# Layer 1's self attention with queries in rows: softmax in rows, probabilities turned by TensorE, three pairs of PSUM banks and a new order in part three

## The chip, the cores and the metric

One core of a Trainium2 chip. The metric is device time in microseconds (us) of one execution. The kernel before takes 1746.66 us, the median of 3 runs (1746.36 to 1750.59).

## The reference, cut to what matters

A decoder of two blocks for 16 sequences of 256 tokens of 128 values, with a second input (a context of 64 tokens of 96 values for each sequence). Every layer adds its result to its input and normalizes the sum. Layer 0 has a causal attention (16 heads of 8), an attention on the context (8 heads of 16) and a mixture of 64 experts; layer 1 has the attention that changes here (16 heads of 64), an attention on the context (16 heads of 64) and a small attention of 8 heads in place of a feed-forward network.

```python
def _L1_attn_ref(x, W_qkv, b_qkv, W_out, b_out):        # x: 16 x 256 x 128
    qkv = (x @ W_qkv + b_qkv).reshape(B, S, 3 * 16, 64)
    Q, K, V = qkv[:, :, :16], qkv[:, :, 16:32], qkv[:, :, 32:]
    scores = jnp.einsum('bqhi,bkhi->bhqk', Q, K) / jnp.sqrt(64.0)
    scores = scores + jnp.triu(jnp.full((S, S), -10000.0), k=1)
    probs = jax.nn.softmax(scores, axis=-1)
    vals = jnp.einsum('bkhi,bhqk->bqhi', V, probs).reshape(B, S, 16 * 64)
    return vals @ W_out + b_out

x = _layernorm(x + _L0_attn_ref(x, ...))
x = _layernorm(x + _L0_xattn_ref(x, ctx_768, ...))
x = _layernorm(x + _L0_ffn_ref(x, ...))
x = _layernorm(x + _L1_attn_ref(x, ...))                 # the layer that changes
x = _layernorm(x + _L1_xattn_ref(x, ctx_768, ...))
x = _layernorm(x + _L1_ffn_ref(x, ...))
```

## The kernel before

**Parts.** Part one is the causal attention and the context attention of layer 0, the router and some folding of weights; part two runs the experts; part three is the whole of layer 1. The change touches part three, and a few constants that are prepared earlier.

**Streams and the written order.** Part three works on two sequences at a time, A and B, in eight repetitions of one body. The work of a body is six streams of steps (`phase3_streams`): for each of the two sequences one of the three layers in a row (`main`), one that sums what the experts left, normalizes it and begins layer 1 for the sequence of the next body (`front`), and one of value projections (`values`). The string `TURNS3` says from which stream the next step is taken, A and B being the main streams, C and D the fronts, E and F the values. `AHEAD3` says how many steps of each stream belong to the next repetition. These ahead steps run for the first bodies in front of the loop, the others of the last bodies behind it. Between lies the loop, from 765.95 to 1688.5 us in the profiled execution, with seven repetitions; in front of it is a stretch from 679.78.

Every engine goes through the same list of steps in the same order (`tensor_step`, `scalar_step`, `vector_step`, `pool_step`, and `transfer_step` for SP, which issues the DMAs), and does its share of each step. An engine that waits in one step holds back all its later steps.

**The steps of layer 1's self attention for one sequence.** XT turns the input. Q and K project queries and keys, two pairs of heads a step; ScalarE adds the bias and writes them, features in rows, to `qt` and `kt`; V projects the values. C casts `qt` (ScalarE) and `kt` (VectorE, L1214) to bf16. There are eight pairs of heads.
- S, eight steps: scores with queries in rows, bf16 (L706) plus a mask (L713), 128x1024 in one pair of PSUM banks; VectorE takes the largest of each row (L1279). They serve only for this maximum. N turns the negated maxima with four small matmuls.
- T, four rounds of two steps: the scores again, now in fp32 with keys in rows (L805), to which a matmul with `shift` (L800) adds the negated maxima and one more (L794) the mask; ScalarE takes the exponential of 128x1024 (L1143) into `prob`.
- P, four steps: the values times the probabilities (L896), and the sums of the probabilities through a matmul with ones (L883) into a bank of its own; ScalarE copies the products (L1150).
- D: VectorE forms the reciprocals of the sums and splits them into three bf16 parts. B, two steps: TensorE spreads them over the features with `spread_b` (L950), and VectorE multiplies the products by them (L1303). W is the output projection (L969), and L the norm.

The context attention of layer 1 (L1X) already has queries in rows in the kernel before: its T steps turn probabilities with eight transposes of 128x128 (L811), and ScalarE copies them (L1134). GpSimd adds the residuals (L1477) and forms the norms' reciprocal roots (L1457, L1460); VectorE applies the norms (L1202).

**PSUM.** `Ledger` hands out units of PSUM in turn from rings. In part three there are six units, two of them pairs of banks (ring Q: S, T and B), one bank for P's products (O), one for the sums (D) and two for all projections (M). In one body Q has 60 fills, M 48, O 10 and D 2. An engine that fills a unit waits until the fill before it is read (`may_fill`).

```python
UNIT_BANK = (0, 2, 4, 5, 6, 7)
RINGS = {"p1": {"Q": (0, 1), "O": (2, 3), "M": (4, 5)},
         "p3": {"Q": (0, 1), "O": (2,), "D": (3,), "M": (4, 5)}}
AHEAD1, AHEAD3 = (22, 17, 6, 0, 0, 0, 0), (16, 22, 15, 15, 4, 4)
```

Of the kernel before, what the change touches and what calls it, by code (L numbers as in the profile page):

```python
# [50 lines left out]
ROUNDS_T = {L0: 4, L0X: 1, L1: 4, L1F: 2}  # L51
# [13 lines left out]
def project_steps(a, s):  # L65
    st = lambda kind, *n: [(kind, a, s, i) for i in n]
    scores = len(S_STEPS[a])
    if a is L1:
        out = st("Q", 0, 1) + st("C", 0) + st("S", 0, 1, 2, 3)
    elif a is L0X:  # L70
        out = st("Q", 0) + st("C", 0) + st("S", 0)
    else:
        out = st("Q", 0) + st("C", 0) + st("S", 0) + st("V", 0) + st("S", *range(1, scores))
    return out + st("N", 0)


def head_steps(a, s):
    out = []
    for g in range(ROUNDS_T[a]):
        out += [("T", a, s, g, k) for k in range(2 if a is L1 else 1)]  # L80
        if g:
            out.append(("P", a, s, g - 1))
# [32 lines left out]
def early_steps(s):  # L115

    st = lambda kind, *n: [(kind, L1, s, i) for i in n]
    return [("XT", L1, s, 0)] + st("K", 0, 1, 2, 3) + st("Q", 2, 3) + st("C", 1) + st("S", 4, 5, 6, 7)


def phase3_streams():
    front = lambda s: [("Z", "F", s, 0), ("Y", "F", s, 0), ("L", "F", s, 0)] + early_steps(s)
    values = lambda s: [("V", L1, s, i) for i in range(4)]
    main = lambda s: (project_steps(L1, s) + head_steps(L1, s)
# [7 lines left out]
TURNS3 = ("B4 A2 D2 A3 D B A B D B D2 A2 B A F B2 A C D5 C F A B A C A B2 A C B D A C5 B A D B2 E A F B3 A B2 "  # L132
          "A2 B2 F A D2 A2 E B E A C A2 B A B A B A C B A B4 A2 B C E B2 A B A B C A2 B C2 A3 B3 A B2 A B2 A B "
          "A B2 A B A B A6 B A B A")
AHEAD1, AHEAD3 = (22, 17, 6, 0, 0, 0, 0), (16, 22, 15, 15, 4, 4)


def interleaved(streams, turns, aheads):
# [16 lines left out]
UNIT_BANK = (0, 2, 4, 5, 6, 7)  # L155
UNITS = len(UNIT_BANK)
RINGS = {"p1": {"Q": (0, 1), "O": (2, 3), "M": (4, 5)},
         "p3": {"Q": (0, 1), "O": (2,), "D": (3,), "M": (4, 5)}}


def fills(step):
# [6 lines left out]
    if kind == "P":  # L168
        if a is L1:
            return ["D", "O"] if step[3] == 0 else ["O"]  # L170
        return ["O"] if step[3] == 0 else []
    if kind == "B":
        return ["Q"]
    if kind in ("D", "E", "L", "C", "CK", "RN", "RL", "Z", "Y") or kind == "W" and step[3]:
        return []
# [3 lines left out]
def tilings(step):  # L179
# [3 lines left out]
    if kind in ("C", "CK", "D", "E", "L", "RN", "RL", "Z", "Y"):  # L183
        return ()
    if kind in ("S", "T") and a in (L0, L1):
        return ((32, 128), (32, 32)) if narrow else ((64, 128), (64, 64))
    if kind in ("S", "T") and a is L1X:
# [3 lines left out]
    if kind == "P":  # L191
        return {L1: ((128, 64), (128, 32)), L0X: ((128, 64),)}.get(a, ((128, 32),))
# [40 lines left out]
def decoder_program(nc, inp, out):  # L233
    ctx = ExitStack()
    with ctx:
# [29 lines left out]
        ones_g = sb("ones_g", [128, 2, 4, 32])  # L265
        spread_b = sb("spread_b", [128, 8, 128], BF16)
        part_cols = sb("part_cols", [128, 2])
# [12 lines left out]
        sel_m = w_early[:, 0:256].bitcast(BF16).rearrange("p (g k) -> p g k", g=4)  # L280
# [7 lines left out]
        peak_w = [w_shared[:, 256 * s:256 * s + 256].bitcast(BF16).rearrange("p (n j c) -> p n j c", n=2, j=2) for s in AB]  # L288
# [41 lines left out]
        qb = pair("qb", [128, 8, T], BF16)  # L330
# [4 lines left out]
        xt_x = [t[:, 0, :] for t in qt]  # L335
        by_query = [[flat(t[:, 4 + 2 * n:6 + 2 * n, :]).rearrange("p (h k) -> p h k", h=16) for n in AB] for t in prob]
# [9 lines left out]
        shift = pair("shift", [128, 2, T], BF16)  # L346
        shift_n = pair("shift_n", [128, 384], BF16)
        rpart = pair("rpart", [128, 128], BF16)
        rdiag = pair("rdiag", [128, 2, 128], BF16)
# [89 lines left out]
        class Sync:  # L439


            def __init__(self, tag):
                n = lambda name: [sem(f"{tag}_{name}{s}") for s in AB]
                self.full = [sem(f"{tag}_full{b}") for b in range(UNITS)]
                self.free = [sem(f"{tag}_free{b}") for b in range(UNITS)]
# [22 lines left out]
                else:  # L468
                    self.fold_in = n("fold_in")
                    self.r_split = n("r_split")  # L470
                    self.r_parts = n("r_parts")
# [5 lines left out]
                    self.f_moments_ready = n("f_moments_ready")  # L477
# [3 lines left out]
                    self.q16_early = n("q16_early")  # L481
                    self.k16_early = n("k16_early")
# [5 lines left out]
        CASTS_K = {L1: 1, L1F: 2}  # L488
# [13 lines left out]
        class View:  # L502
# [28 lines left out]
            def bank(self, step, i=0):  # L531
                return psum[:, UNIT_BANK[ledger[self.tag].use[step, i][0]], :]

            def pair(self, step, i=0):
                b = UNIT_BANK[ledger[self.tag].use[step, i][0]]
# [28 lines left out]
            def q_cast(self, a, s):  # L564
                return self.count([("C", x, s, 0) for x in LAYERS[self.tag] if x is not L1X], ("C", a, s, 0))

            def k_cast(self, a):
                return self.at(1, 1) if self.tag == "p1" else self.at(2, CASTS_K[a])

# [8 lines left out]

            def wide(self, n):
                return self.at(3, 1 + n)  # L580
# [36 lines left out]
        def tensor_step(pe, v, step):  # L617
# [31 lines left out]
            elif kind == "K":  # L649
# [6 lines left out]
                else:  # L656
                    if i == 0:
# [23 lines left out]
            elif kind == "S":  # L681
# [4 lines left out]
                elif step[3] == 0:  # L686
# [3 lines left out]
                    else:  # L690
                        pe.wait_ge(y.k16[s], v.k_cast(a))
                if a is L1 and which == 4:
                    pe.wait_ge(y.q16_early[s], v.once())
                    pe.wait_ge(y.k16_early[s], v.once())
# [1497 lines left out]
```

## Time and profile before

| | |
|---|---|
| median of 3 runs | 1746.66 us (1746.36 to 1750.59) |
| profiled execution, span | 1784.5 us |
| TensorE busy | 1570.9 us, 88% (16,544 matmuls) |
| VectorE busy | 1115.2 us, 62% |
| ScalarE busy | 837.8 us, 47% |
| GpSimd busy | 243.8 us, 14% |
| mean granted TensorE clock | 0.966 of full speed |

The busy times come from one profiled execution, whose own time is its span of 1784.5 us. Busy time is the time in which an engine works at instructions; matmuls overlap, and what is counted is the time that they cover together. The granted clock is the share of full speed that TensorE was allowed. Shares of the whole span mix the three parts, which have different limits; the rows further down are of part three alone unless they say otherwise.

### The profile page before, as it was taken

Reading aid. Unit: us, or ns where it says so; the run is one execution under the profiler, and the core shown is the slowest. Engines: PE = TensorE matmul, PEld = TensorE weight load, DVE = VectorE, ACT = ScalarE, POOL = GpSimd, SP = SyncE. Lnnn points to the kernel's source line nnn. Section 1 sums busy time; section 2 is a strip of 40 time slices with the busy share of each in tenths; the row PEclk is TensorE's granted clock in tenths of the full one; section 3 lists DMA queues with packets and bytes.
Section 4 is the critical chain, followed back from the end, with each engine's and each line's share of the span. In section 5 each row is a group of like instructions: output and inputs, shape, how many; then the busy total and the mean of one; then the engine's idle time right before and its main releaser. Section 6 shows DMA issues by size and latency. Waiting matters only on the chain.

```text
span 1784.5 us, 39554 instructions
## 1 busy us (share of the span) xinstructions
PE 1570.9 (88%) x16544; PEld 1003.6 (56%) x16544; DVE 1115.2 (62%) x2227; ACT 837.8 (47%) x1516; POOL 243.8 (14%) x404
## 2 busy tenths in 40 slices
PE   4899889998853887999999999999999999999975
PEld 2555555555532764565565565665665665665653
DVE  5187777877751345377477388388388387298264
ACT  1565565556530223436436445545545445455433
POOL 1011110111006240011011011011011011011011
PEclk9999999999976889999999999999999999999988
DMA  8521111111139243011011011011010010000000
GB/s 274 203 74 51 54 54 61 65 46 48 49 119 110 48 125 105 1 37 52 9 37 54 8 38 53 8 53 37 8 60 31 8 60 31 8 24 28 5 1 7
DMA packets 64993, 95.58 MB, mean 54 GB/s; under 512 B 9425, under 2 KB 47298, under 8 KB 64083
## 3 DMA queue, kind: packets, MB, share of 16 engines
q1 hardware_dynamic: 61491, 89.20, 14.9%
q0 software_dynamic: 2560, 3.46, 2.2%
q8 instruction: 134, 2.20, 0.5%
q10 hardware_dynamic: 768, 0.40, 0.1%
q14 instruction: 40, 0.33, 0.1%
HBM read 56.03 MB, written 38.80 MB: 53 GB/s over the span
## 4 chain that ended last, share of the span: by engine, by line
PE 62%; DVE 21%; ACT 7%; issue 5%; another core or an unknown queue 2%; POOL 2%; ACTq 0%; DVEq 0%; DMA 0%; POOLq 0%; PEldq 0%
PE psum L805 6%; PE psum L896 6%; PE psum L646 5%; PE psum L883 4%; PE psum L717 3%; DVE w_shared L1279 2%; PE psum L976 2%; PE psum L969 2%; PE psum L800 2%; PE psum L661 2%; ACT prob L1143 2%; PE psum L854 2%; PE psum L923 2%; PE psum L671 2%
## 5 line engine op out<-in xcount | busy, mean ns | idle before, releaser
L1143 ACT ACTIVATE prob<-psum 128x1024 f32<-128x1024 f32 (+1 forms) x320 | 290.0, 937 | 223.3 <-PE psum L794 95.1
L1279 DVE TENSOR_REDUCE w_shared<-psum 128x4 bf16<-128x1024 f32 x128 | 153.0, 1224 | 129.2 <-PE psum L713 95.7
L1457 POOL TENSOR_TENSOR rstd<-moments,eps 128x2 f32<-128x2 f32 x64 | 15.4, 241 | 1004.0 <-DVE moments L1188 1004.0
L1279 DVE TENSOR_REDUCE kt<-psum 128x4 bf16<-128x1024 f32 (+2 forms) x112 | 132.1, 1215 | 10.4 <-PE psum L738 10.4
L805 PE MATMUL psum<-qt,kt 64*128 64x256 f32 x1024 | 131.4, 376 | 0.0
L896 PE MATMUL psum<-prob,v_big 128*64 128x256 f32 x1024 | 124.6, 385 | 0.0
L805 PEld LDWEIGHTS psum<-qt,kt 64*128 64x128 f32 x1024 | 98.7, 189 | 9.9
L1303 DVE TENSOR_TENSOR qt<-qt,psum 128x1024 f32<-128x1024 f32 x32 | 39.0, 1218 | 90.3 <-PE psum L950 89.8
L923 PE MATMUL psum<-prob,va 128*32 128x256 f32 (+1 forms) x1536 | 91.3, 356 | 1.2 <-ACT prob L1143 1.1
L896 PEld LDWEIGHTS psum<-prob,v_big 128*64 128x64 f32 x1024 | 67.8, 136 | 43.1 <-ACT prob L1143 8.0
L1279 DVE TENSOR_REDUCE va<-psum 128x4 bf16<-128x1024 f32 x64 | 77.4, 1219 | 7.9 <-PE psum L750 6.9
L1150 ACT COPY qt<-psum 128x512 f32<-128x512 f32 x64 | 37.6, 587 | 80.2 <-PE psum L896 80.2
L646 PE MATMUL psum<-xt,w_late 128*128 128x256 f32 x256 | 68.4, 406 | 2.4 <-PEq L1043 1.2
L671 PE MATMUL psum<-w_late,xt 128*128 128x512 f32 x128 | 68.6, 620 | 2.0 <-PEq L1043 1.0
L883 PE MATMUL psum<-prob,ones_g 128*32 128x128 f32 x2048 | 67.5, 275 | 0.0
L1071 ACT ACTIVATE qt<-psum,b_qk 128x256 f32<-128x256 f32 x128 | 53.0, 476 | 30.7 <-PE psum L646 29.9
L1084 ACT ACTIVATE kt<-psum,b_qk 128x256 f32<-128x256 f32 x128 | 53.8, 471 | 28.7 <-PE psum L661 27.5
L661 PE MATMUL psum<-xt,w_late 128*128 128x256 f32 x256 | 64.9, 397 | 1.1 <-ACT xt L1062 0.6
L883 PEld LDWEIGHTS psum<-prob,ones_g 128*32 128x32 f32 x2048 | 52.5, 109 | 21.5 <-issue 21.5
L923 PEld LDWEIGHTS psum<-prob,va 128*32 128x32 f32 x1536 | 40.8, 110 | 42.3 <-issue 16.4
L969 PE MATMUL psum<-w_late,qt 128*128 128x128 f32 x512 | 61.9, 277 | 2.5 <-DVE qt L1303 2.5
L976 PEld LDWEIGHTS psum<-w_late,prob 128*128 128x128 f32 x512 | 59.6, 192 | 7.6 <-issue 7.6
(325 smaller groups left out, 3259.9 us busy)
## 6 DMA issues: line engine op xcount, KB each, us to landing
zd<-kx SPq DMA_DIRECT2D x24, 512.0 KB, 6.0
union<-zd SPq DMA_DIRECT2D x16, 768.0 KB, 4.3
w_late<-ad SPq DMA_DIRECT2D x16, 512.0 KB, 3.7
w_late<-vd SPq DMA_DIRECT2D x16, 512.0 KB, 4.6
ad<-union SPq DMA_DIRECT2D x16, 256.0 KB, 2.1
vd<-union SPq DMA_DIRECT2D x16, 256.0 KB, 2.2
xg<-union SPq DMA_DIRECT2D x16, 192.0 KB, 1.9
w_late<-in_w1T SPq DMA_DIRECT2D x1, 2816.0 KB
```

Of the source, the lines that this page charges most:

```text
L646: last = mm(bank[:, j * 256:(j + 1) * 256], w[:, c * 128:(c + 1) * 128], x, start=True, stop=True)
L661: last = mm(bank[:, j * 256:(j + 1) * 256], w1_qkv[:, c * 128:(c + 1) * 128], xt[s][:, :], start=True, stop=True)
L671: last = mm(bank[:, :], xt[s][:, t * 128:(t + 1) * 128], w1_qkv[:, 2048 + 512 * half:2560 + 512 * half], start=True, stop=True)
L805: last = mm(banks[:, u, j * 256:(j + 1) * 256], kt[s][r, c, ktile * 128:(ktile + 1) * 128], qt[s][r, c, :], start=False, stop=turned, skip ...
L883: last = mm(sums[r:r + 32, 0:128], ones_g[:, u, g, :], prob[s][:, slot + 2 * k + u, c:c + 128], start=(g == 0 and k == 0 and u == 0), stop ...
L896: last = mm(bank[64 * u:64 * u + 64, j * 256:(j + 1) * 256], v_big[s][:, k, h * 64:(h + 1) * 64], prob[s][:, slot + 2 * k + u, j * 256:(j ...
L923: last = mm(bank[32 * j:32 * j + 32, c + q0:c + 256], lhs, p, start=(g == 0 and k == 0), stop=(k == 1), skip_group_check=True)
L969: last = mm(bank[:, t * 128:(t + 1) * 128], qt[s][:, u, t * 128:(t + 1) * 128], w1_o[:, u, :], start=(u == 0 and t == 0), stop=(u == 7), s ...
L976: last = mm(bank[:, t * 128:(t + 1) * 128], by_key[s][t][:, 128 * u:128 * u + 128], vw_x[s][:, u, :], start=(u == 0 and t == 0), stop=(u = ...
L1084: last = nc.scalar.activation(kt[s][:, c, :], bank[:, j * 256:(j + 1) * 256], ACT.Identity, bias=b1_qk[:, 8 + c:9 + c])
L1143: nc.scalar.activation(prob_of[a][s][:, slot + 2 * i:slot + 2 * i + 2, 0:n], v.pair(step, i)[:, :, 0:n], ACT.Exp, scale=a.scale).then_inc( ...
L1279: nc.vector.tensor_reduce(dst, src, axis=AX.X, op=ALU.max).then_inc(v.free(step), 1)
```

## The change

Layer 1's self attention is written anew, with queries in rows throughout.
- **S** multiplies `qt` and `kt` in fp32 instead of their bf16 copies (the factor 0.125 is now in the queries, their bias and the mask). VectorE takes the negated maxima of the rows, and ScalarE takes the exponentials straight from these scores, in four instructions of 128x256 (a half of the queries and a head each) with the negated maximum as bias and the sum of each row as a second result.
- **E**, new: VectorE forms the reciprocals of the four columns of sums, and GpSimd multiplies the 128x1024 probabilities by them.
- **T** turns these with eight transposes of 128x128 in place of building the scores again; the copy out of PSUM is VectorE's for four pairs of heads and ScalarE's for the other four.
- **P** works on one pair of heads a step, and two steps share one fill of a bank. The sums through ones, and the steps D, B, N and C of this layer, are gone. W waits for ScalarE's copies of P.
- **Pairs of heads** come in the order 4, 5, 6, 7, 0, 1, 2, 3; two of them start in the front stream.
- **PSUM**: ring Q has three pairs of banks, ring M the two other banks; P's products fill M. In one body Q has 56 fills and M 56.
- **Order**: a new `TURNS3`, and `AHEAD3` is (33, 0, 14, 10, 4, 2).
- **Constants**: `ones_g`, `spread_b` and `part_cols` are no longer loaded, `sel_m` and `shift` no longer prepared; `b1_qk` is loaded earlier and scaled.

```diff
-ROUNDS_T = {L0: 4, L0X: 1, L1: 4, L1F: 2}
+ROUNDS_T = {L0: 4, L0X: 1, L1F: 2}
+PAIR_ORDER = (4, 5, 6, 7, 0, 1, 2, 3)
+TURNED_BY_VECTOR = (4, 6, 0, 2)
...
+def pair_steps(s):
+    st = lambda kind, *n: [(kind, L1, s, PAIR_ORDER[i]) for i in n]
+    out = st("S", 2) + st("E", 2) + st("T", 0) + st("S", 3) + st("E", 3) + st("P", 0)
+    for i in range(4, len(PAIR_ORDER)):
+        out += st("T", i - 3) + st("S", i) + st("E", i) + st("P", i - 3)
+    return out + st("T", 5) + st("P", 5) + st("T", 6) + st("P", 6) + st("T", 7) + st("P", 7)
...
-        out = [("D", a, s, 0), *meanwhile, ("B", a, s, 0), ("B", a, s, 1), ("W", a, s, 0), ("W", a, s, 1)]
+        out = [("W", a, s, 0), *meanwhile, ("W", a, s, 1)]
...
-    return [("XT", L1, s, 0)] + st("K", 0, 1, 2, 3) + st("Q", 2, 3) + st("C", 1) + st("S", 4, 5, 6, 7)
+    return (st("XT", 0) + st("K", 2) + st("Q", 2) + st("S", 4) + st("E", 4) + st("K", 3) + st("S", 5) + st("E", 5)
+            + st("Q", 3) + st("K", 0, 1))
...
-AHEAD1, AHEAD3 = (22, 17, 6, 0, 0, 0, 0), (16, 22, 15, 15, 4, 4)
+AHEAD1, AHEAD3 = (22, 17, 6, 0, 0, 0, 0), (33, 0, 14, 10, 4, 2)
...
-UNIT_BANK = (0, 2, 4, 5, 6, 7)
+UNIT_BANK = {"p1": (0, 2, 4, 5, 6, 7), "p3": (0, 2, 4, 6, 7)}
...
-         "p3": {"Q": (0, 1), "O": (2,), "D": (3,), "M": (4, 5)}}
+         "p3": {"Q": (0, 1, 2), "M": (3, 4)}}
...
# tensor_step, S
-                                    last = mm(banks[:, u, 256 * n:256 * n + 256], qb[s][r, which, q0:q0 + 128],
-                                              kb[s][r, which, :], start=(n == 0 and not turned), stop=(n == 1 and turned),
+                                    last = mm(banks[:, u, 256 * n:256 * n + 256], qt[s][r, which, q0:q0 + 128],
+                                              kt[s][r, which, :], start=(n == 0 and not turned), stop=(n == 1 and turned),
# tensor_step, T of L1
+                    rows = rows_l1[s][PAIR_ORDER.index(g) % 4]
+                    for k in range(2):
+                        for u in range(2):
+                            for t in range(2):
+                                o, c = 256 * u + 128 * t, 512 * u + 256 * (1 - t) + 128 * k
+                                last = nc.tensor.transpose(banks[:, k, o:o + 128], rows[:, c:c + 128], ident[:, :])
# tensor_step, P of L1
+                    fill, j = ("P", a, s, g - g % 2), g % 2
+                    keys = keys_l1[s][PAIR_ORDER.index(g) % 2]
+                    if j == 0:
+                        pe.wait_ge(*v.may_fill(fill))
+                    bank = v.bank(fill)
                     for k in range(2):
+                        for u in range(2):
+                            h = 2 * g + u
+                            last = mm(bank[64 * u:64 * u + 64, j * 256:(j + 1) * 256], v_big[s][:, k, h * 64:(h + 1) * 64],
+                                      keys[:, k, 256 * u:256 * u + 256], start=(k == 0), stop=(k == 1))
+                    if j == 1:
+                        last.then_inc(v.full(fill), 1)
# scalar_step
+            elif kind == "S" and a is L1:
+                c = step[3]
+                rows, banks = rows_l1[s][PAIR_ORDER.index(c) % 4], v.pair(step)
+                act.wait_ge(y.peaks[s], v.pair_of_heads("S", s, c))
+                for u in range(2):
+                    for n in range(2):
+                        o = 512 * u + 256 * n
+                        last = nc.scalar.activation(rows[:, o:o + 256], banks[:, u, 256 * n:256 * n + 256], ACT.Exp,
+                                                    bias=negative_peak[s][:, c, u, n:n + 1],
+                                                    accum_out=row_sum[s][:, c, u, n:n + 1])
                 last.then_inc(v.free(step), 1)
# vector_step
+            elif kind == "E" and a is L1:
+                c = step[3]
+                dve.wait_ge(*v.drained(("S", L1, s, c)))
+                nc.vector.reciprocal(row_sum[s][:, c, :, :], row_sum[s][:, c, :, :]).then_inc(y.divisors[s], 1)
+            elif kind == "T" and a is L1:
+                if step[3] in TURNED_BY_VECTOR:
+                    dve.wait_ge(*v.filled(step))
+                    nc.vector.tensor_copy(flat(keys_l1[s][PAIR_ORDER.index(step[3]) % 2]), flat(v.pair(step))).then_inc(
+                        v.free(step), 1)
...
+                    nc.vector.tensor_reduce(negative_peak[s][:, which, :, :], banks.rearrange("p u (n k) -> p u n k", n=2),
+                                            axis=AX.X, op=ALU.max, negate=True).then_inc(y.peaks[s], 1)
# pool_step
+            if kind == "E" and a is L1:
+                c = step[3]
+                pool.wait_ge(y.divisors[s], v.pair_of_heads("E", s, c))
+                rows = rows_l1[s][PAIR_ORDER.index(c) % 4].rearrange("p (n k) -> p n k", n=4)
+                by = row_sum[s][:, c, :, :].rearrange("p u n -> p (u n)").unsqueeze(2).to_broadcast([128, 4, T])
+                nc.gpsimd.tensor_tensor(rows, rows, by, ALU.mult).then_inc(y.rows_ready[s], 1)
```

## Rows read from the trace of the kernel before

**Rows 1.** Windows: stretch, length, busy PE, PEld, DVE, ACT, POOL, clock, DMA share, GB/s.
```profile
1170.04:1301.82 131.78, 126.30 (x1240) 80.51 (x1244) 87.17 (x149) 65.66 (x106) 14.21 (x28) 1.00 0.10 33
1171.99:1255.31 83.32, 77.93 (x590) 48.59 (x591) 72.62 (x121) 43.51 (x81) 13.20 (x26) 1.00 0.13 47
679.78:765.95 86.17, 77.04 (x709) 44.15 (x709) 35.01 (x49) 38.32 (x62) 2.31 (x4) 0.93 0.08 24
1688.50:1784.50 96.00, 64.73 (x540) 43.58 (x532) 50.33 (x93) 28.72 (x44) 11.09 (x22) 0.86 0.01 4
```

**Rows 2.** Timeline of TensorE in the loop: start, us, engine, line, operation, tiles, count.
```profile
1243.61 0.39 PE L706 MATMUL psum<-kb,qb 64*128 64x256 bf16 x4
...
1244.71 1.07 PE L923 MATMUL psum<-prob,va 128*32 128x256 f32 x16
...
1253.43 0.39 PE L800 MATMUL psum<-shift,sel_h 64*128 64x512 bf16 x2
...
1257.89 1.03 PE L805 MATMUL psum<-qt,kt 64*128 64x256 f32 x8
1258.85 1.95 PE L896 MATMUL psum<-prob,v_big 128*64 128x256 f32 x16
1260.73 1.08 PE L883 MATMUL psum<-prob,ones_g 128*32 128x128 f32 x32
1261.74 0.39 PE L706 MATMUL psum<-kb,qb 64*128 64x256 bf16 x4
```

**Rows 3.** Lines of one repetition, TensorE: group, count | busy, mean ns | idle before.
```profile
L950 PE MATMUL psum<-rdiag,spread_b 128*128 128x256 bf16 x16 | 2.4, 274 | 0.9 <-DVE rdiag L1296 0.9
```

**Rows 4.** Timeline of TensorE, layer 1's context attention, in the loop and behind it.
```profile
1210.65 1.04 PE L811 MATMUL psum<-ident,prob 128*128 128x128 f32 x8
1211.52 1.02 PE L671 MATMUL psum<-w_late,xt 128*128 128x512 f32 x2
...
1718.12 1.91 PE L811 MATMUL psum<-ident,prob 128*128 128x128 f32 x8
```

**Rows 5.** Lines of one repetition, ScalarE.
```profile
L1143 ACT ACTIVATE prob<-psum 128x1024 f32<-128x1024 f32 x24 | 24.1, 1023 | 20.0 <-PE psum L794 11.9 <-PE psum L805 6.1 <-PE psum L854 2.0
...
L1134 ACT COPY prob<-psum 128x1024 f32<-128x1024 f32 x4 | 4.0, 1004 | 3.6 <-PE psum L811 3.5
```

**Rows 6.** Timeline of ScalarE in part one, the router's exponentials with row sums.
```profile
116.79 0.31 ACT L1172 ACTIVATE qt<-psum,qt 128x64 f32<-128x64 f32 x1 [0.52 <-DVE qt L1346]
117.00 0.19 ACT L1172 ACTIVATION_READ_ACCUMULATOR qt<-psum,qt 128x1 f32 x1
117.09 0.30 ACT L1172 ACTIVATE qt<-psum,qt 128x64 f32<-128x64 f32 x1
```

**Rows 7.** Lines of one repetition, VectorE.
```profile
L1279 DVE TENSOR_REDUCE w_shared<-psum 128x4 bf16<-128x1024 f32 x16 | 19.1, 1224 | 14.6 <-PE psum L713 10.4 <-PE psum L706 4.1
...
L1303 DVE TENSOR_TENSOR qt<-qt,psum 128x1024 f32<-128x1024 f32 x4 | 4.9, 1218 | 11.2 <-PE psum L950 11.1
...
L1214 DVE CAST kb<-kt 128x1024 bf16<-128x1024 f32 x4 | 2.7, 684 | 0.0
```

**Rows 8.** Lines of part three's middle, 800 to 1680 us, GpSimd.
```profile
L1477 POOL TENSOR_TENSOR x_res<-x_in,b_o 128x256 f32<-128x256 f32 x14 | 10.2, 726 | 0.0
...
L1457 POOL TENSOR_TENSOR rstd<-moments,eps 128x2 f32<-128x2 f32 x40 | 7.9, 197 | 535.3 <-DVE moments L1188 535.3
```

**Rows 9.** Timeline of GpSimd and VectorE in part one.
```profile
149.37 0.72 POOL L1477 TENSOR_TENSOR x_res<-union,b_o 128x256 f32<-128x256 f32 x1
149.54 0.89 DVE L1202 TENSOR_SCALAR x_tok<-summed,moments,rstd 128x128 f32<-128x128 f32 x2 [0.78 <-POOL rstd L1460]
150.35 1.21 DVE L1219 TENSOR_TENSOR kt<-qt,slot_mask 128x1024 f32<-128x1024 f32 x1
150.51 1.65 POOL L1477 TENSOR_TENSOR v_big<-x_tok,bx_o 128x256 f32<-128x256 f32 x1 [0.42 <-DVE x_tok L1202]
```

**Rows 10.** The chain that ended last, in order of time: start, us, what.
```profile
7.79 5.23 DMA prob<-in_tri
```

More of the change, by code:

```diff
@@ L79, in head_steps @@
     for g in range(ROUNDS_T[a]):
-        out += [("T", a, s, g, k) for k in range(2 if a is L1 else 1)]
+        out.append(("T", a, s, g))
         if g:
@@ L685, in tensor_step @@
                     pe.wait_ge(y.fold_in[s], v.at(32, 32))
-                elif step[3] == 0:
+                elif a is L1:
+                    pe.wait_ge(*v.drained(("Q", a, s, which // 2)))
+                    pe.wait_ge(*v.drained(("K", a, s, which // 2)))
+                elif step[3] == 0 and not a.big:
                     pe.wait_ge(y.q16[s], v.q_cast(a, s))
@@ L690, in tensor_step @@
                     else:
[L691 to L694, printed above, removed]
+                        pe.wait_ge(y.k16[s], v.once())
                 pe.wait_ge(*v.may_fill(step))
@@ L744, in tensor_step @@
                                 last = mm(banks[:, jj, :].rearrange("p (i k) -> p i k", i=heads.stop - heads.start),
-                                          qb[s][r, 0, q0:q0 + 128], kb[s][r, heads, keys], start=not turned, stop=turned,
+                                          qb[s][r, 0, q0:q0 + 128], kb_of[a][s][r, heads, keys], start=not turned, stop=turned,
                                           skip_group_check=True)
@@ L943, in tensor_step @@
                 last.then_inc(v.full(step), 1)
-            elif kind == "B":
-                i, banks = step[3], v.pair(step)
-                if i == 0:
-                    pe.wait_ge(y.r_parts[s], v.wide(0))
-                pe.wait_ge(*v.may_fill(step))
-                for j in range(4):
-                    last = mm(banks[:, j // 2, (j % 2) * 256:(j % 2) * 256 + 256], spread_b[:, 4 * i + j, :],
-                              rdiag[s][:, :, :], start=True, stop=True)
-                last.then_inc(v.full(step), 1)
             elif kind == "W":
@@ L955, in tensor_step @@
                 bank = v.bank(whole)
-                before = ("B" if a is L1 else "T", a, s, step[3]) if a.big else ("A2", a, s, 0)
-                if a.big or not v.follows(step, before):
-                    pe.wait_ge(*v.drained(before))
+                if a is L1:
+                    for n in range(2):
+                        pe.wait_ge(*v.drained(("P", a, s, 4 * step[3] + 2 * n)))
+                elif a is L1X:
+                    pe.wait_ge(*v.drained(("T", a, s, step[3])))
+                elif not v.follows(step, ("A2", a, s, 0)):
+                    pe.wait_ge(*v.drained(("A2", a, s, 0)))
                 if step == whole:
@@ L1147, in scalar_step @@
                 if a is L1:
-                    fill = step, 1 if g == 0 else 0
-                    act.wait_ge(*v.filled(*fill))
-                    copy(flat(qt[s][:, 2 * g:2 * g + 2, :]), v.bank(*fill)).then_inc(v.free(*fill), 1)
+                    if g % 2 == 1:
+                        fill = ("P", a, s, g - 1)
+                        act.wait_ge(*v.filled(fill))
+                        copy(flat(qt[s][:, g - 1:g + 1, :]), v.bank(fill)).then_inc(v.free(fill), 1)
                 elif g == ROUNDS_T[a] - 1:
@@ L2050, in _ @@
             for y in (p1, p3):
[L2051 to L2052 removed]
+                for free in y.free:
+                    dve.sem_inc(free, 1)
             dve.sem_inc(p1.sorted, 1)
```

320 lines of the change are left out of this document (96 added, 224 removed).

## The prediction

> **What bounds the kernel now.** First the busy time by stretch [rows 1]. One repetition of part three's loop (two sequences) takes 131.78 us and TensorE is busy for 126.30 of it at full granted clock; VectorE has 87.17, ScalarE 65.66, GpSimd 14.21. So part three is TensorE's, 5.5 us idle in each repetition. The next row of the group shows that VectorE is not free either: for 83.32 us of the repetition it is busy for 72.62, and in the rest it has almost nothing to do. The last two rows are the ends: before the loop 86.17 us with 77.04 of TensorE, after it 96.00 with 64.73, at granted clocks of 0.93 and 0.86. Then TensorE in order of time [rows 2]: a step's cost is read from its start to the next step's start, since the ends overlap. Part three is 1104.5 us, from 679.8 to the end of the span at 1784.5; it is eight times 126.3 (1010.4), 7 times 5.5 of idle (38.4), and 55.7 that the ends lose, to waiting and to the lower clock.
>
> **The change, part by part: TensorE, for one sequence's layer-1 attention.**
> Taken away. Eight T steps rebuild the scores with keys in rows: from the first L800 at 1253.43 to the L896 at 1258.85 are four of them, 5.42 us, so 10.8 for eight [rows 2]. Four P steps: L896 takes 1.88 (1258.85 to 1260.73) and the sums over ones, L883, 1.01, so 11.6. Eight S steps in bf16: two in 1.10 (1243.61 to 1244.71), so 4.4. The two B steps: 2.4 us in a repetition, 1.2 a sequence [rows 3]. The four small matmuls of N are left out. Sum 28.0.
> Added. S now multiplies qt and kt in fp32 in the shape of L805, eight instructions of 64x256: 0.96 (1257.89 to 1258.85) [rows 2]. The mask stays; I take it as half of the old S, 0.27. Eight S: 9.8. T is eight transposes of 128x128, the work of L811: 0.87 from 1210.65 to 1211.52 [rows 4], eight T: 7.0. P keeps the 16 instructions of L896 for every two pairs of heads, 0.94 a pair, 7.5. Sum 24.3.
> So 3.7 to 4.0 us a sequence; with N, and with the changes of array shape inside P that go, I take 4.0: 8.0 a repetition, 64 over eight. TensorE then needs 118.3 us.
>
> On the transposes: those of L811 took 0.87 us at full clock and 1.91 at the lower one [rows 4], so they run with the granted clock. The Trainium skill (TensorE: Matmul & The Clock Gate, Part 4: PE-mode transpose) says that the full clock is not granted for transposes; by it the 7.0 us would be twice that. The row at 1210.65 disagrees, but there the eight stand alone between matmuls, and the new kernel has 128 of them in each repetition. It is a rival below.
>
> **ScalarE.** Sixteen exponentials of 128x1024 at 1.023 leave a repetition [rows 5]. 64 of 128x256 come, each with a sum by row. Such a sum is a second instruction: at 64 columns the two start 0.30 apart from the next two (116.79 to 117.09) [rows 6]. From 64 columns (0.31) to 1024 (1.02) a column costs 0.74 ns, so 0.30 + 0.14 = 0.44, four to a pair of heads: 1.8 us. If nothing overlapped it were 0.31 + 0.14 + 0.19 = 0.64, or 2.6. I take 1.9, nearest to rows that stand back to back. Half of the turned probabilities are copied here, 8 at 1.0 [rows 5]. Sum 65.7 - 16.4 + 30 + 8 = 87 of some 128, the casts that go left in as a margin. It is hidden as work; as a wait it isn't, see VectorE.
>
> **VectorE.** Gone in a repetition: four products L1303 and four casts L1214, 4.9 + 2.7 [rows 7], and D, not counted. Added: 8 copies of 128x1024 from PSUM, for which I take the reduction's 1.22 (the cast's 0.68 is the other end): 9.8, and 16 reciprocals of four columns, some 0.2 each. Sum 87.2 - 7.6 + 9.8 + 3 = 92. But each reciprocal waits for the four exponentials of its pair, and all of VectorE's later work stands behind it: the next reduction, T's copies, the norms. Reduction 1.22, exponentials 1.9, some 0.25 for handing over: for about 9 of the 16 pairs the order puts less than the 2.15 us of waiting between the two, and I count 11 us of waiting in all. Lane: 92 + 11 = 103, and at VectorE's own density in its full stretch (83.32 for 72.62 [rows 1]) the 92 become 106 and the lane 117: level with TensorE's 118.
>
> **GpSimd.** It gets 16 products of 128x1024. An addition of 256 columns takes 0.726 and one of 2 takes 0.197 [rows 8]: 2.08 ns a column, 2.33 us for 1024, 37 in a repetition; with the old 14 it is busy for 0.40 of the time. T waits for it: reduction to product some 6.2 us after S; TensorE has at least 9 us of other steps between an S and its T, so a quiet chain hides. Upper end: the addition that met a VectorE product took 1.65, 0.92 more [rows 9]; at 1.7 times the price 3.9 us.
> The rows of that group show what the two engines do to each other. At 149.54 VectorE's two scalings, which began in the midst of a GpSimd addition, took 0.89 and ended with 0.34 after it; the addition that began at 150.51, behind VectorE's product of 150.35, took 1.65 and ended 0.60 after that product. Each was held until the other had finished. With GpSimd at work for 0.40 of the time, and 1.2 us as half of a product, each group of scalings or of products of two SBUF tensors on VectorE loses 0.48; I count 18 (eight norms, four in L1X's softmax, Z, Y and C of both sequences): 8.6 us in a repetition. At 3.9 us and a share of 0.6 they are 21. The Trainium skill (SBUF — State Buffer, on the shared port pair) has this as an exclusive lock for the whole instruction, which the trace bears out; by it the new products are what VectorE must now wait behind.
>
> **PSUM and the order.** S and T now rotate over three pairs of banks, and P shares two banks with all projections; P holds one of them from one pair of heads to the next. Where a fill of the same bank follows soon (XT of A behind P 5 of B) it waits for ScalarE's copy, up to 1.6 us when four exponentials stand ahead. SP's loads are issued at the same kinds of steps, and each still has more than half a repetition (some 60 us) before its data is used: nothing. GpSimd's norms stand behind products: in the 0.48 above.
>
> **Sum of a repetition.** TensorE 118.3. Idle: 5.5 before, less 0.9 that was the wait for D [rows 3]; A's six pairs in a row, where VectorE's lane has some 4.6 us a pair and TensorE 4.0, 3.5 together; for B's half, the shared bank and the norms behind GpSimd 2. That is 10, so 128.3, 3.5 less than now.
> The ends: A's attention now runs almost alone ahead of the loop, and B's last two layers alone behind it, so less work overlaps; but there is less of it, and the order ahead is shorter. I take 50 for the 55.7, between 40 and 75.
> Part three: 946.4 + 70 + 50 = 1066, 38 less. At the start three constants are no longer loaded, while VectorE and GpSimd wait for a DMA that is 5.23 us of the chain [rows 10]: between 0 and 5, I take 1. So 39 to 40 us less.
> The profiled execution's own time is given by its span alone, 1784.5 us; the median of the runs is 1746.66, 37.8 lower, and so the extra lies in the profiled execution. In part three's loop the clock is full, and I take the difference over unchanged: 1746.7 - 39.6 = 1707.
>
> **The rivals.**
> *TensorE's idle stays as it is* (6 us a repetition, ends 40): 946 + 42 + 40, 76 less, 1670. For it: three engines have room on average. Against: VectorE's lane at 117.
> *VectorE's lane becomes the period.* Its place is the reciprocal behind the exponentials, with GpSimd's products holding the rest. With 2.6 us of exponentials (18 of waiting), 3.9 us products (21): 106 + 18 + 21 less the handing over that the density already holds, 139. Then 946 + 7 x 20.7 + 56 = 1147: 42 more, 1788. It decides from a repetition of about 134 on. Against it: the middle values give 117 + 9.
> *Nothing gained*: a repetition of 132 to 134, between the two, 1735 to 1752.
> *Transposes at the lower clock.* By the row at 1718.12 they cost 0.84 to 1.04 more each step, some 6.8 us a sequence: 109 more in all, 1816. The row at full clock speaks against it.
>
> **How the numbers follow.** The forecast (1685 to 1735) 0.5; idle as before 0.2; VectorE's lane 0.18; nothing gained 0.09; transposes 0.03. Low end 1660, high end 1762: below it lies all but the outer part of the slow cases. This kernel's measurement can tell 0.3% from no change, 5.2 us. Faster 0.76, same 0.06, slower 0.18.
>
> **What would show it.** Right: a repetition of 126 to 131 with TensorE busy for some 118; eight transposes in 0.87; four exponentials and their reads in 1.8 to 2.0; products on GpSimd near 2.3; VectorE's reciprocals waiting for ScalarE. Wrong: a repetition above 134 with VectorE without gaps (the lane), products above 3 us, or a granted clock below 1 inside the loop. If TensorE's busy time falls by much more or less than 8 us, the step costs were misread.

## The result, and the profile after

The changed kernel takes 1753.47 us (median of 16 runs, 1746.31 to 1769.96), the kernel before 1746.36 (median of 16, 1740.35 to 1760.76): a ratio of 1.0049, 95% interval 1.003 to 1.0067. It is slower by about 7 us, where 39.6 us less were forecast.

Three stretches of part three after, against [rows 1]. Columns as there.

```profile
636.33:709.05 72.72, 55.65 (x341) 34.73 (x341) 27.80 (x42) 34.96 (x112) 18.50 (x12) 0.92 0.08 26
...
1628.50:1753.80 125.30, 85.03 (x592) 55.70 (x592) 61.76 (x109) 46.99 (x107) 25.84 (x32) 0.84 0.01 4
1103.00:1234.10 131.10, 123.45 (x924) 80.80 (x924) 91.95 (x153) 80.67 (x218) 44.72 (x44) 1.00 0.10 33
```

The last row is one repetition: 131.10 us, where 131.78 stood before; TensorE is busy for 123.45 (126.30 before) and waits for 7.65 (5.5 before). The stretch in front of the loop (first row) fell from 86.17 to 72.72, the one behind it grew from 96.00 to 125.30. Together the two ends have 57.3 us without TensorE; before they had 40.4.

Now the whole. Part three runs from 636.3 to the end of the span at 1753.8, 1117.5 us; before it took 1104.7. Eight times 123.45 is 987.6. The seven repetitions take 131.46 each on average (the step that opens the loop starts at 709.05 and, seven repetitions on, at 1629.30), so 7 x 8.0, 56.1, is waiting. 73.8 is left for the ends. Against [rows 1] that is 22.8 less work, 17.7 more waiting in the loop and 17.8 more at the ends.

The start is earlier by 3.4 us, one execution against one (in the other seven profiled executions of the new kernel and its variants the same matmuls start at 71.4 to 73.2). In the chain of waits in order of time (start, us, what) the same matmuls of part one stand after, then before, at

```profile
7.79 3.03 DMA prob<-in_tri
...
73.43 3.78 PE psum L1862 x32
```

```profile
76.79 3.78 PE psum L1934 x32
...
558.31 21.83 another core or an unknown queue
```

The second row of the kernel before is the largest of four such waits in part two, 40.3 us together, about the 38 us by which its profiled execution was longer than its median; the chain of after has none, as the prediction assumed. So 12.8 more in part three less 3.4 is 9.4; the profiled execution of after (1755.88) lies 2.4 above its median, which leaves the 7.

The price of a step is seen in TensorE's timeline (columns as in [rows 2]; the first of the sizes, such as 128*64, is the shape of the part of TensorE's array that the instruction uses, called its array shape below):

```profile
1109.93 1.04 PE L785 MATMUL psum<-ident,kb 128*128 128x128 f32 x8
1110.80 0.38 PE L634 MATMUL psum<-ident,x_tok 128*128 128x128 f32 x2
...
1115.24 1.08 PE L856 MATMUL psum<-prob,v_big 128*64 128x256 f32 x8
1116.26 1.09 PE L785 MATMUL psum<-ident,qb 128*128 128x128 f32 x8
1117.28 1.13 PE L710 MATMUL psum<-kt,qt 64*128 64x256 f32 x8
1118.35 0.36 PE L717 MATMUL psum<-w_early,ident_add 64*64 64x384 bf16 x4
```

Eight transposes took 0.87 from 1109.93, behind and ahead of steps of their own array shape (128*128), as in [rows 4]. From 1116.26, between steps of two other shapes, they took 1.02. P took 1.02 here (0.94 was taken), S 1.07 (0.96 was taken). Summed by line over the repetition from 1103.63 to 1234.72, from each start to the next and without the idle time that the rows show, the sixteen steps of each kind cost: T 16.5 us, P 16.2, S 17.05 and its mask 4.6. That is 54.3; the prediction had 48.6.

### The profile page after: what moved, and what is told of

The parts are those of the page before. It is cut to its first block, busy times and chain, and to the rows that moved or that the text cites. A ratio compares the mean times of both kernels' runs of the same rounds, so it can differ in the third digit from the quotient of the medians.

```text
span 1753.8 us, 35652 instructions
## 1 busy us (share of the span) xinstructions
PE 1543.1 (88%) x14032; PEld 1005.1 (57%) x14048; DVE 1148.2 (65%) x2246; ACT 958.4 (55%) x2412; POOL 485.2 (28%) x527
## 3 DMA queue, kind: packets, MB, share of 16 engines
q8 instruction: 115, 1.88, 0.4%
## 4 chain that ended last, share of the span: by engine, by line
PE 62%; DVE 23%; ACT 7%; issue 5%; POOL 2%; DMA 1%; ACTq 0%; DVEq 0%; POOLq 0%; PEld 0%; PEldq 0%
PE psum L710 6%; PE psum L856 5%; PE psum L785 4%; PE psum L650 4%; PE psum L930 4%; PE psum L923 3%; PE psum L675 3%; PE psum L833 3%; PE psum L882 2%; DVE negative_peak L1219 2%; PE psum L721 2%; PE psum L790 2%; PE psum L717 2%; PE psum L665 2%; DVE kx L1337 2%
## 5 line engine op out<-in xcount | busy, mean ns | idle before, releaser
L1219 DVE TENSOR_REDUCE negative_peak<-psum 128x4 f32<-128x1024 f32 x128 | 155.7, 1217 | 130.2 <-PE psum L717 121.3
L1095 ACT ACTIVATE prob<-psum 128x768 f32<-128x768 f32 (+1 forms) x192 | 158.8, 879 | 101.8 <-PE psum L816 61.3
L1075 ACT ACTIVATE prob<-psum,negative_peak 128x256 f32<-128x256 f32 x256 | 117.9, 473 | 101.4 <-DVE negative_peak L1219 101.4
L1401 POOL TENSOR_TENSOR prob<-prob,row_sum 128x1024 f32<-128x1024 f32 x64 | 121.2, 1894 | 152.5 <-DVE row_sum L1200 152.5
L710 PE MATMUL psum<-kt,qt 64*128 64x256 f32 x1024 | 145.8, 403 | 3.6 <-ACT prob L1075 1.6
L710 PEld LDWEIGHTS psum<-kt,qt 64*128 64x128 f32 x1024 | 89.8, 187 | 39.7 <-issue 28.4
L1075 ACT ACTIVATE qb<-psum,negative_peak 128x256 f32<-128x256 f32 x128 | 59.0, 472 | 65.3 <-DVE negative_peak L1219 65.3
L1204 DVE COPY prob<-psum 128x1024 f32<-128x1024 f32 x64 | 77.2, 1206 | 10.7 <-PE psum L785 10.7
L1075 ACT ACTIVATE kb<-psum,negative_peak 128x256 f32<-128x256 f32 x128 | 59.0, 477 | 33.0 <-DVE negative_peak L1219 33.0
L1089 ACT COPY prob<-psum 128x1024 f32<-128x1024 f32 x64 | 65.1, 1017 | 21.6 <-PE psum L785 20.9
L665 PE MATMUL psum<-xt,w_late 128*128 128x256 f32 x256 | 69.1, 400 | 4.1 <-ACT xt L1016 2.8
L785 PE MATMUL psum<-ident,prob 128*128 128x128 f32 x512 | 69.5, 279 | 0.0
```

Source lines behind the costliest of these rows:

```text
L665: last = mm(bank[:, j * 256:(j + 1) * 256], w1_qkv[:, c * 128:(c + 1) * 128], xt[s][:, :], start=True, stop=True)
L710: last = mm(banks[:, u, 256 * n:256 * n + 256], qt[s][r, which, q0:q0 + 128], kt[s][r, which, :], start=(n == 0 and not turned), stop=(n = ...
L785: last = nc.tensor.transpose(banks[:, k, o:o + 128], rows[:, c:c + 128], ident[:, :])
L1075: last = nc.scalar.activation(rows[:, o:o + 256], banks[:, u, 256 * n:256 * n + 256], ACT.Exp, bias=negative_peak[s][:, c, u, n:n + 1], ac ...
L1095: nc.scalar.activation(prob_of[a][s][:, slot + 2 * i:slot + 2 * i + 2, 0:n], v.pair(step, i)[:, :, 0:n], ACT.Exp, scale=a.scale).then_inc( ...
L1204: nc.vector.tensor_copy(flat(keys_l1[s][PAIR_ORDER.index(step[3]) % 2]), flat(v.pair(step))).then_inc(v.free(step), 1)
```

## The experiments

Theory 1, formed on these rows: TensorE still sets the repetition, and the new steps cost more than they were priced, because nearly all of the 48 stand alone between steps of another array shape. Theory 2: VectorE's lane sets it (the reciprocals behind the exponentials, and what GpSimd's products hold up). Theory 3: TensorE's instructions are slower because the other engines use the memories more. Where one run was made, its repetition in the profile is compared, not its time.

**Every T and P issued twice in a row.**

```diff
-                    for k in range(2):
-                        for u in range(2):
-                            for t in range(2):
+                    for n in range(16):
+                        k, u, t = n // 4 % 2, n // 2 % 2, n % 2
...
-                    for k in range(2):
-                        for u in range(2):
+                    for n in range(8):
+                        k, u = n // 2 % 2, n % 2
```

> Theory 1 (lone steps): the new S, T and P steps cost TensorE about 0.1 us more than the rows of before because each stands alone between steps of another array shape. Here the eight transposes of every T and the eight matmul instructions of every P are issued twice in a row, with the same result. By theory 1 the second half has a neighbour of its own shape and costs the old price: 0.87 for the transposes, 0.94 for P, so T's step goes from 1.03 to 1.90 and P's from 1.01 to 1.95, and a repetition (131.1 now) gets up to 29 us longer: 153 if the 7 us in which TensorE waits take some of it, 160 if not. Theory 3 (crowding): TensorE's instructions are slower because the other engines read and write the same memories more; then the second half costs as much as the first, 2.06 and 2.02 a step, and 32.6 us a repetition.

TensorE's timeline, and the window of one repetition:

```profile
1216.27 1.95 PE L855 MATMUL psum<-prob,v_big 128*64 128x256 f32 x16
1218.15 1.97 PE L784 MATMUL psum<-ident,kb 128*128 128x128 f32 x16
1220.04 1.13 PE L710 MATMUL psum<-kt,qt 64*128 64x256 f32 x8
...
1335.26 1.98 PE L675 MATMUL psum<-w_late,xt 128*128 128x512 f32 x4
1337.08 1.91 PE L784 MATMUL psum<-ident,kb 128*128 128x128 f32 x16
1338.82 0.38 PE L634 MATMUL psum<-ident,x_tok 128*128 128x128 f32 x2
```

```profile
1204.94:1356.99 152.05, 149.93 (x1182) 103.95 (x1180) 90.52 (x153) 81.46 (x219) 44.75 (x44) 1.00 0.09 29
```

P takes 1.88 and T 1.89 where the two stand singly at 1.02. Over all sixteen, T went from a mean of 1.03 to 1.84 and P from 1.01 to 1.88: the second half costs 0.81 and 0.86. Theory 3, by which both halves cost as much as a single step does now, is out. The repetition grew by 21 us, a little less than theory 1 had (152.05, where 153 to 160 was expected): 26.8 us of work came in, and TensorE's waiting fell from 7.65 to 2.1.

What the array shape has to do with it is seen in T. The step at 1337.08 stands between steps of T's own shape and takes 1.74; the same step of the changed kernel, at 1109.93, takes 0.87. There both halves cost 0.87, the price that the prediction took. So a neighbour of another shape is worth up to 0.16 of T's mean of 1.03. The 0.22 between 1.03 and 0.81 is too much: some of the single steps end in short waits that are not listed as idle time (0.13 behind the T at 1137.55), and doubling hides these. P's 0.15 rests on doubling alone: no single P stands beside another step of its shape, so what any step costs at its start is not told apart from the shape there. S was not doubled. Its price of 0.96 came from a step that follows its own shape and is followed by another, and now it has its own on neither side (1.07); in the kernel before, L805 between two L800 of its own shape took 0.86 where nothing held it up:

```profile
1255.19 1.03 PE L805 MATMUL psum<-qt,kt 64*128 64x256 f32 x8
1256.05 0.39 PE L800 MATMUL psum<-shift,sel_h 64*128 64x512 bf16 x2
```

So S's 0.11 fits the same cause, read from rows and not from a run.

The Trainium skill (TensorEngine Tiling (Array Packing), Key Properties) says that a change of tiling mode, in difference to a change of tile, drains the TensorE. The T steps here agree with it (0.87 between steps of their own shape, 1.03 on average), and it is the rule that spoke against the prediction's prices; the section gives no figure for it.

**No division.** Reciprocals and products are left out; T waits for the exponentials.

```diff
-                nc.vector.reciprocal(row_sum[s][:, c, :, :], row_sum[s][:, c, :, :]).then_inc(y.divisors[s], 1)
...
-                nc.gpsimd.tensor_tensor(rows, rows, by, ALU.mult).then_inc(y.rows_ready[s], 1)
...
-                    pe.wait_ge(y.rows_ready[s], v.pair_of_heads("E", s, g))
+                    pe.wait_ge(*v.drained(("S", L1, s, g)))
```

> Leaves out the division of the probabilities by their sums (VectorE's reciprocals and GpSimd's products); T waits for the exponentials alone. Theory 1 (lone steps): TensorE's busy time in a repetition stays at 123 to 124.5 us, and of the 7 us in which it waits some 2 to 4 go: a repetition of 126 to 129. Theory 2 (lane): the reciprocals behind the exponentials and the products that hold VectorE set the 131.1; then nearly all of the waiting goes, and the repetition falls below 126. Theory 3 (crowding by GpSimd): TensorE's busy time falls to the 118 to 120 that the old step prices give.

```profile
1107.34:1235.03 127.69, 122.65 (x926) 80.87 (x925) 85.52 (x137) 80.60 (x219) 14.17 (x28) 1.00 0.10 34
```

The repetition fell by 3.4 to 127.69, inside theory 1's range. TensorE's busy time hardly moved (122.65, just under the 123 to 124.5 that theory 1 had, and far from theory 3's 118 to 120), so GpSimd's work does not make the matmuls much slower; TensorE's waiting fell from 7.65 to 5.0. The division's path is worth 3.4 us a repetition, and is not what sets the period. What GpSimd's products do to VectorE is seen in its lines over the loop, first of after, then of this run (group, count | busy, mean ns | idle before):

```profile
L1149 DVE TENSOR_SCALAR x_norm<-summed,moments,rstd 128x128 f32<-128x128 f32 x28 | 29.2, 1082 | 0.0
...
L1167 DVE TENSOR_TENSOR kx<-qt,slot_mask 128x512 f32<-128x512 f32 x14 | 18.6, 1330 | 21.0 <-ACT qt L1025 21.0
...
L1260 DVE TENSOR_SCALAR x_in<-x_in,moments_f,rstd_f 128x128 f32<-128x128 f32 x28 | 16.8, 639 | 0.0
```

```profile
L1167 DVE TENSOR_TENSOR kx<-qt,slot_mask 128x512 f32<-128x512 f32 x14 | 9.7, 693 | 35.6 <-ACT qt L1025 35.6
L1259 DVE TENSOR_SCALAR x_in<-x_in,moments_f,rstd_f 128x128 f32<-128x128 f32 x28 | 8.3, 339 | 0.0
L1149 DVE TENSOR_SCALAR x_norm<-summed,moments,rstd 128x128 f32<-128x128 f32 x28 | 8.3, 339 | 0.0
```

On average a scaling of 339 ns became one of 1082, a product of 693 one of 1330. The timeline of the changed kernel shows two scalings that began in the midst of one product on GpSimd and ended 0.09 us after the next product:

```profile
1145.30 1.90 POOL L1401 TENSOR_TENSOR prob<-prob,row_sum 128x1024 f32<-128x1024 f32 x1
...
1145.81 3.33 DVE L1149 TENSOR_SCALAR x_norm<-summed,moments,rstd 128x128 f32<-128x128 f32 x2
1147.15 1.90 POOL L1401 TENSOR_TENSOR kb<-kb,row_sum 128x1024 f32<-128x1024 f32 x1
```

Per repetition these three lines lose 4 x 0.74, 2 x 0.64 and 4 x 0.30, 5.4 us. VectorE as a whole loses less: its busy time fell by 6.4 us without the division, and 2.7 of that are the reciprocals themselves. So the holding that the prediction read from [rows 9], and put at 8.6 us, is real but smaller, and TensorE's work covers most of it: with the waiting for the reciprocals it is worth at most the 3.4.

**All copies of T on ScalarE.**

```diff
-TURNED_BY_VECTOR = (4, 6, 0, 2)
+TURNED_BY_VECTOR = ()
```

> All copies of the turned probabilities go to ScalarE, so VectorE loses 8 copies of 1.21 us a repetition (9.7 us of 92) and ScalarE gets 8 of 1.02. Theory 1 (TensorE sets the repetition by its own steps and the order): 130.5 to 132.5, no gain. Theory 2 (VectorE's lane sets it): at least 3 us less, 128 or below.

Two repetitions in one window:

```profile
990.47:1253.35 262.88, 247.87 (x1849) 162.27 (x1849) 165.29 (x288) 174.68 (x453) 89.82 (x88) 0.99 0.10 33
```

131.4 us each, with VectorE busy for 82.6 in place of 91.95 and ScalarE, which now makes the copies, for 87.3 in place of 80.7. Taking 9 us off VectorE gains nothing. As ScalarE is loaded in exchange, this alone would not settle it; together with the run without division, which loads no engine and stayed above theory 2's 126, theory 2 falls.

**Two pairs of PSUM banks, as before the change.**

```diff
-UNIT_BANK = {"p1": (0, 2, 4, 5, 6, 7), "p3": (0, 2, 4, 6, 7)}
+UNIT_BANK = {"p1": (0, 2, 4, 5, 6, 7), "p3": (0, 2, 4, 5, 6, 7)}
...
-         "p3": {"Q": (0, 1, 2), "M": (3, 4)}}
+         "p3": {"Q": (0, 1), "M": (2, 3, 4, 5)}}
```

> The rings of PSUM as before the change: two pairs of banks for S and T and four single banks, with the new attention and order as they are. A pair is held for some 4.6 us by an S step (1.36 of matmuls, 1.22 of reduction, 1.94 of exponentials) and 2.3 by a T. If the third pair is what the new attention lives on, TensorE waits for pairs: a repetition of 136 to 146 us. If the single banks were the shorter side, it gets faster than 131; if PSUM plays no part, 131 within 1 us.

Two repetitions, and the three largest of TensorE's waits in one of them (us in total, times, longest):

```profile
1191.23:1495.02 303.79, 260.73 (x1850) 170.18 (x1849) 182.71 (x305) 161.99 (x437) 89.32 (x88) 0.96 0.09 29
```

```profile
PE psum L785 <- ACT prob L1075: 3.7, 3, 1.4
PE psum L790 <- ACT qb L1075: 2.3, 1, 2.3
PE psum L710 <- ACT kb L1075: 2.2, 3, 0.9
```

151.9 us each, beyond the range: the price was underestimated. T (L785; L790 is the context attention's) and S (L710) now wait for the exponentials (L1075) that hold a pair; these three waits are 8.2 of some 21 us. With this order, which was made for three pairs, the third pair is worth 20 us a repetition, so the new rings are no mistake.

**Another order of the same steps.**

```diff
-AHEAD1, AHEAD3 = (22, 17, 6, 0, 0, 0, 0), (33, 0, 14, 10, 4, 2)
+AHEAD1, AHEAD3 = (22, 17, 6, 0, 0, 0, 0), (33, 0, 14, 12, 4, 2)
...
-TURNS3 = ("D B D B2 F2 C B2 A D B C A B4 C A B A B D C B A C2 A B4 A2 B C B4 A B3 E B C A B A C A B A B A4 B C "
+TURNS3 = ("B3 F C B D A B2 F C A B4 C A2 B2 C B D A C2 A B4 A2 B3 C B2 A B3 E B A C B A C A2 B2 A2 B A C A B A "
...
```

> The changed kernel with another written order (TURNS3, and AHEAD3 (33, 0, 14, 12, 4, 2)), all else as it is. The order was sought by adding up the trace's own step durations through many orders; for this one the sum is 128.8 us a repetition (131.1 now), with the head of part three some 8 us shorter: about 1725 us. Theory 1: the 7 us in which TensorE waits in a repetition come from where steps stand (a norm, a cast, a product that is just late), so another order gets 2 to 3 of them back with TensorE's busy time the same, 1720 to 1732, faster than the kernel before. Theory 2 (VectorE's lane sets the repetition): no order of the same steps helps, 131 and 1750. A still runs its attention ahead of B here, so the tail should stay near 125 us.

```profile
981.00:1110.35 129.35, 123.84 (x928) 81.09 (x924) 87.82 (x153) 80.37 (x219) 44.23 (x44) 1.00 0.10 34
```

1727.87 us (6 runs) beside 1743.19 for the kernel before: 0.9918 of it, 0.9897 to 0.9938. TensorE is as busy as before (123.84), its waiting fell to 5.5, and the repetition to 129.35. Theory 1 expected that. With this order the new attention beats the old one, in the old one's own order, by 15 us; the order of the change cost it about 1.3%, some 23 us. Of this the profiled executions show 20 in part three, which takes 1097.5 us (628.96 to 1726.5) in place of 1117.5: 5.8 in front of A's first output projection, 14.1 in the loop, and nothing behind A's last one, where 54.4 us are left with either order. Part three of the kernel before took 1104.7, 7.2 more, and the matmuls of part one at 76.79 stand at 71.40 here, so the profiles show 12.6 of the 15. The rest lies in the parts in front, which vary: part three begins between 627.95 and 638.60 in the eight profiled executions of the new kernel and its variants.

**The masked block left out.** The queries 0 to 127 don't see the keys 128 to 255, so a quarter of S's scores is masked away, and a quarter of what T turns and P multiplies is zeros. The edit shortens all that handles this block, on the other engines too (not shown). First with the order as it is, then with an order sought for it.

```diff
-                                    last = mm(banks[:, u, 256 * n:256 * n + 256], qt[s][r, which, q0:q0 + 128],
-                                              kt[s][r, which, :], start=(n == 0 and not turned), stop=(n == 1 and turned),
+                                    k = 128 + q0
+                                    last = mm(banks[:, u, 256 * n:256 * n + k], qt[s][r, which, q0:q0 + 128],
+                                              kt[s][r, which, 0:k], start=(n == 0 and not turned), stop=(n == 1 and turned),
...
-                            for t in range(2):
-                                o, c = 256 * u + 128 * t, 512 * u + 256 * (1 - t) + 128 * k
+                            for t in range(k, 2):
+                                o, c = 128 * u if k else 256 * u + 128 * t, 512 * u + 256 * (1 - t) + 128 * k
...
```

> The changed kernel, order as it is; S, T, P, the exponentials, the reduction, the product and the copies leave out the block of queries 0 to 127 by keys 128 to 255, which the mask of -10000 makes exactly zero. By the prices of e1_twice (0.81 for eight transposes alone and 0.22 for standing alone, 0.86 and 0.15 for P) T falls by 0.20, P by 0.21, S and its mask by some 0.28: 11 us a repetition. Theory 1 (TensorE's steps set the repetition): 119 to 122 and 1655 to 1670 us. Theory 2 (VectorE's lane): two shorter reductions in place of one and three quarters of a copy give it only some 5 us, so the repetition stays above 125 and the time above 1700.

> c1_causal with an order sought for its step durations in the same way (AHEAD3 (33, 2, 14, 12, 4, 2)): the sum gives 117.9 us a repetition and about 25 us less than c1_causal in all, 1630 to 1645. Where VectorE's lane sets the repetition, no less than c1_causal.

One repetition of the first, then of the second:

```profile
961.92:1082.69 120.77, 112.59 (x894) 77.31 (x893) 85.00 (x169) 75.68 (x218) 40.15 (x60) 1.00 0.11 36
```

```profile
964.90:1084.89 119.99, 113.44 (x895) 77.55 (x893) 81.50 (x169) 74.92 (x218) 39.75 (x60) 1.00 0.11 36
```

The first takes 1664.21 us, 0.9558 of the kernel before (0.953 to 0.9586), and a repetition of 120.77: TensorE's work fell by 10.9 us and the repetition by 10.3. T and P cost 0.80 a step, as the prices of the first experiment give (0.83 and 0.80). VectorE's busy time fell by 7.0, less than the repetition did. That is theory 1 once more: what leaves TensorE leaves the repetition. The second, 1658.71 us (0.951, 0.9485 to 0.9535), is the fastest of all, but misses its number by 14 us at least: the repetition came to 120.0 and not 117.9, with 6 us of waiting spread over many small ones that were not followed further.

## Why the prediction was wrong, step by step

**TensorE's work is the step that failed.** What is taken away was right: 28.0 us a sequence were counted, and the lines of before add up to 28.5. What is added was priced at 24.3 a sequence and costs 27.2. The prices came from rows in which a step had a neighbour of its own array shape: the transposes of [rows 4] at 0.87, S as L805 behind L800 in [rows 2], and P as half of a step of twice the length. In the new kernel nearly all of the 48 new steps of a repetition stand singly. Over a repetition T came out 2.5 us dearer than priced, S with its mask 2.0, and P 1.2; the runs show the cause for T and P, and for S it is read from rows. "The changes of array shape inside P that go" were even booked as a gain; in fact the repetition still has 94 changes from one shape to the next between neighbouring rows of TensorE's timeline, and had 98. So TensorE's busy time fell by 2.85 us a repetition and not by 8: 22.8 in all in place of 64, a miss of 41.

**The ends are the second.** 50 was taken (40 to 75), 74 came. The last matmuls of a sequence are its last output projection. In TensorE's timeline those of A and B stand, after (L918) and then before (L964), at

```profile
1699.35 0.66 PE L918 MATMUL psum<-wf_o,vx 128*64 128x128 f32 x8 [0.46 <-ACT vx L1110]
...
1745.15 0.66 PE L918 MATMUL psum<-wf_o,vx 128*64 128x128 f32 x8 [0.46 <-ACT vx L1110]
```

```profile
1765.88 0.66 PE L964 MATMUL psum<-wf_o,vx 128*64 128x128 f32 x8
...
1775.59 0.66 PE L964 MATMUL psum<-wf_o,vx 128*64 128x128 f32 x8 [0.46 <-ACT vx L1157]
```

They are 45.8 us apart after and 9.7 before.

The windows around and behind A's last one (the columns of [rows 1]) show what is left:

```profile
1690.00:1705.00 15.00, 9.71 (x81) 5.47 (x82) 9.20 (x15) 6.08 (x8) 0.72 (x1) 0.93 0.00 0
1705.00:1720.00 15.00, 8.59 (x47) 7.76 (x45) 5.48 (x16) 2.61 (x4) 2.98 (x7) 0.72 0.04 10
1720.00:1735.00 15.00, 8.02 (x38) 4.01 (x38) 5.82 (x7) 3.41 (x9) 0.92 (x2) 0.50 0.00 0
1735.00:1753.80 18.80, 6.98 (x66) 3.58 (x66) 2.44 (x9) 4.34 (x6) 0.91 (x2) 0.68 0.03 8
```

From there on only the rest of B's last two layers runs: TensorE is busy for about half of the time, at a granted clock that falls as far as 0.50, its lower level (1.2 GHz). The prediction named this ("B's last two layers alone behind it") and then counted on there being less work, which is not what such a stretch costs. That the order's offset between A and B is the cause is read from these rows and not shown by a run: no order with the two in step was run.

**TensorE's waiting** was overestimated: 10 us a repetition were taken, 7.65 to 8 came, 14 us less in all. **The start** gave 3.4 where 1 was taken. 41 and 24 less 14 and 2.4 is 48.6; less the 2.4 by which the profiled execution lies above its median it is 46.2, and between 1707 and 1753.5 are 46.5. (Two slips in the prediction's sum are of no weight here: part three before took 1104.7 and not 1104.5, so its ends took 56.0 and not 55.7, and its terms add up to 39.1 less and not 39.6.)

**The other engines were near.** VectorE was given 92 us a repetition and has 91.95. In part that is luck: by the run without division some 3.7 of these are time in which GpSimd's products hold it, which the prediction counted apart from the 92. ScalarE was given 87 and has 80.7; four exponentials with their sums 1.9 us, and they take 1.81 from the first to what follows:

```profile
1109.49 0.47 ACT L1075 ACTIVATE prob<-psum,negative_peak 128x256 f32<-128x256 f32 x1 [1.78 <-DVE negative_peak L1219]
...
1111.30 0.38 ACT L1016 COPY qt<-psum 128x256 f32<-128x256 f32 x1
```

A copy of 1024 columns out of PSUM on VectorE takes 1.21 (1.22 was taken), a GpSimd product 1.89 to 2.01 (2.33). The reciprocals wait for 7.7 us a repetition (11), as the line says (busy, mean ns | idle before):

```profile
L1200 DVE RECIPROCAL row_sum<-row_sum 128x4 f32<-128x4 f32 x16 | 2.7, 171 | 7.7 <-ACT qb L1075 4.0 <-ACT prob L1075 2.9 <-ACT kb L1075 0.8
```

**The rivals.** The time fell beside "nothing gained" (1735 to 1752), whose repetition of 132 to 134 did not come true: it is 131.1. VectorE's lane as the period is refuted by the copies on ScalarE and by the run without division. Transposes at the lower clock are refuted by the granted clock of 1.00 in the repetition, with 128 new transposes in it. The rule of the Trainium skill that the prediction weighed (TensorE: Matmul & The Clock Gate, Part 4: PE-mode transpose) is thus not borne out for transposes that stand among matmuls; no run here has a stretch of transposes alone.

## What to carry to other kernels

Price a step of a few small matmuls by rows in which it stands between the neighbours that it will have: beside steps of another array shape they cost some 0.15 us more here, about 15% of such a step. Where one engine is busy for 94% of a repetition, as here, relief for the others is worth little and work taken from that engine shows nearly in full; look first for work that multiplies zeros. And a gain per repetition is to be set against the ends: with seven repetitions, the ends of this order, which puts one stream 33 steps ahead of the other, took 18 us more than before, and another written order of the same steps turned 7 us lost into 15 gained.

## What was not expected of the hardware

A step of eight transposes took 0.87 us between steps of its own array shape and 1.03 on average, nearly always beside another shape; a step of P took 1.01 alone, and 0.86 behind another P. GpSimd's product of 1024 columns, with one operand broadcast, took 1.89 us, where the line through the additions of 256 and 2 columns of [rows 8] had given 2.33. And a VectorE scaling of 339 ns took 1082 on average with such products on GpSimd.
